# Four attentions of a transformer kernel: one counter for each cleared buffer, GpSimd's clears behind VectorE's first norms, and the centring of one weight moved to an earlier stage

## The chip, the cores and the metric

The kernel runs on 1 core of one Trainium2 chip. A core has five engines, each with an instruction stream of its own: TensorE (matmuls and transposes, results in PSUM), VectorE, ScalarE, GpSimd (which doesn't reach PSUM here) and SyncE (which issues DMAs). They are synchronised by semaphores alone: an instruction increments one when it is done, another engine waits until it has reached a number. The metric is the device time of one execution in microseconds.

## What is computed

A small vision transformer: 32 images, 25 tokens each, 192 channels, 12 heads of 16. A tokenizer makes the tokens, then four pairs of blocks follow, each with a residual and a LayerNorm. Four blocks matter here; they are cut to their core:

```python
# L1_ffn and L3_ffn: attention whose q, k, v projection has low-rank adapters, 2 of 8 chosen for each token
router_probs = softmax(x_flat @ W_gate.T + b_gate); top_k_weights, top_k_indices = top_k(router_probs, 2)
a_down = einsum('td,nrd->tnr', x_flat, A)
qkv = x @ W_qkv.T + b_qkv + sum over the chosen of weight * (a_down @ B_lora) * scaling
attn = softmax(q @ k.T * scale); return (attn @ v) @ W_proj.T + b_proj
...
# L2_attn: no bias in qkv, and q and k are normed for each head
def _norm_unbiased(t):
    mu = t.mean(-1); var = ((t - mu) ** 2).sum(-1) / (d - 1); return (t - mu) / sqrt(var)
q = _norm_unbiased(q); k = _norm_unbiased(k)
attn = softmax(q @ k.T * scale); return (attn @ v) @ proj_w.T + proj_b
...
# L3_attn: plain attention with biases
h = _layernorm(h + block(h))      # around each block
```

The subtraction of the mean in `_norm_unbiased` is done on the weights: since q and k are linear in x without a bias, centring each head's 16 columns of the weight centres every q and k.

## The kernel before

The program is nine stages, one after another. Each is a `tw.stage`, at whose end the stage's semaphores are cleared and all engines meet in a barrier (line 84). Stage 4 is L1_ffn, stage 5 L2_attn, stage 6 a mixture of experts (L2_ffn), stage 7 L3_attn, stage 8 L3_ffn. The function `attention` is called four times: as "adapted" for stages 4 and 8, as "unit" for stage 5 and as "biased" for stage 7.

The residual `tw.y` lies in SBUF as 8 tiles of 128 rows (4 images of 32 rows, 25 of them tokens). An attention handles them in four pairs, software-pipelined by one loop over i on each engine; the order on each engine is as the code is written.

- **Norm.** In a unit or biased stage VectorE norms tile t (`norm(t)`, line 759, `tensor_scalar` from `tw.y` into h): tiles 0 and 1 first, then it clears hT's rows behind the channels (line 764), sets one of them to ones (766), does the same for outT (774, 776), and then enters the loop, where the norms of later tiles are. TensorE transposes h (615), ScalarE stores the transposed tokens into hT (878; it waits for `ones_ready` 1), and TensorE projects q and k (628) and v (670). In an adapted stage a function `front` has normed and transposed all tiles before (2045, 2065, 2081), for the routing.
- **Adapters.** In an adapted stage TensorE first multiplies with the adapters' `down` weights (623, into bank_b), VectorE multiplies the result with the routing weights into mixT (785, `mix_adapters`), and the projections read mixT.
- **Clears.** Buffers whose padding must be zero are cleared by GpSimd at the start of each of these stages: qT (961), v_heads (962), probs (963), and mixT (965) in an adapted stage or top (967) in the others. All count up one semaphore, `cleared`, and whoever writes into one of these buffers first waits for `cleared` 4: VectorE in `mix_adapters`, `store_values` (818, v_heads) and `shift` (825, top and probs), ScalarE in `store_queries` (906, 907, qT) and `store_values` (916, v_heads). In a unit stage VectorE writes qT (801, 802), and GpSimd has one further job, a product into kd (974).
- **Centring.** In the unit stage VectorE centres the weights w["qk"] in place, between the memsets of hT and outT (769, 771, 773). TensorE's first projection there waits for `centred` 3.
- **Keys.** kd holds k times a mask of heads (789): from PSUM in adapted and biased stages, from SBUF in the unit stage.

`front` of stage 4 has this order on VectorE: eight norms, then a wait for TensorE's routing logits, then their copy (2048). Its SyncE queue loads expert weights of stage 6 meanwhile (fetch).

The functions that the diff touches:

Of the kernel before, what the change touches and what calls it, by code (L numbers as in the profile page):

```python
# [525 lines left out]
def attention(tw, name, kind, w, given=None):  # L526
# [12 lines left out]
    ones_ready, cleared, centred = tw.sem(name + "_ones"), tw.sem(name + "_cleared"), tw.sem(name + "_centred")  # L539
# [11 lines left out]
    with ExitStack() as ctx:  # L551
# [11 lines left out]
        if unit:  # L563
            mean = sb("w_mean", [HALF, HALVES * 2 * HEADS])
            square = sb("square", [P, 2, 3, PAIR_TOKENS])
            inv_std = sb("inv_std", [P, 2, 3, PAIR_TOKENS])
            k_unit = sb("k_unit", [P, 2, 2, PAIR_TOKENS])
# [39 lines left out]
        def _(pe):  # L607
# [25 lines left out]
            def project_queries_keys(f):  # L633
# [4 lines left out]
                if unit:  # L638
                    pe.wait_ge(centred, 3)
# [117 lines left out]
        def _(dve):  # L757
# [9 lines left out]
            if unit:  # L767
                by_head = w["qk"][0:HALF].rearrange("q k (h d) -> q (k h) d", d=HEAD_DIM)
                nc.vector.tensor_reduce(mean[:], by_head, AX_X, ALU.add).then_inc(centred, 1)
                dve.wait_ge(centred, 1)  # L770
                nc.vector.tensor_scalar(mean[:], mean[:], 1.0 / HEAD_DIM, None, ALU.mult).then_inc(centred, 1)
                dve.wait_ge(centred, 2)
                nc.vector.tensor_tensor(by_head, by_head, mean[:].unsqueeze(2).to_broadcast([HALF, HALVES * 2 * HEADS, HEAD_DIM]), ALU.subtract).then_inc(centred, 1)
# [4 lines left out]
            def mix_adapters(f):  # L778
                dve.wait_ge(down_in_psum, f + 1)
                dve.wait_ge(cleared, 4)  # L780
# [11 lines left out]
            def store_keys(f):  # L792
# [4 lines left out]
                if unit:  # L797
                    dve.wait_ge(inverse, 2 * f + 2)
                    nc.vector.tensor_tensor(k_unit[:, f % 2, 0], ps_k[0], inv_std[:, f % 2, 1], ALU.mult).then_inc(k_first, 1)
                    nc.vector.tensor_tensor(k_unit[half:P, f % 2, 1], ps_k[1], inv_std[half:P, f % 2, 2], ALU.mult).then_inc(k_scaled, 1)  # L800
                    nc.vector.tensor_tensor(qT[:, f % 2, 0, :, 0:TOKENS], by_image(ps_q[0]), by_image(inv_std[:, f % 2, 0]), ALU.mult)
# [9 lines left out]
            def store_values(t):  # L811
                dve.wait_ge(v_in_psum, t + 1)
                dve.wait_ge(cleared, 4)
# [7 lines left out]
            def shift(t):  # L821
                dve.wait_ge(scores_in_psum, t + 1)
                dve.wait_ge(cleared, 4)
# [47 lines left out]
        def _(act):  # L871
# [29 lines left out]
            def store_queries(f):  # L901
                act.wait_ge(a_in_psum, f + 1)
                act.wait_ge(cleared, 4)
# [5 lines left out]
            def store_values(t):  # L909
                act.wait_ge(v_in_psum, t + 1)  # L910
                act.wait_ge(cleared, 4)
# [48 lines left out]
        def _(pool):  # L960
            nc.gpsimd.memset(qT[:], 0.0).then_inc(cleared, 1)
            nc.gpsimd.memset(v_heads[:], 0.0).then_inc(cleared, 1)
            nc.gpsimd.memset(probs[:], 0.0).then_inc(cleared, 1)
            if adapted:
                nc.gpsimd.memset(mixT[:], 0.0).then_inc(cleared, 1)
            else:
                nc.gpsimd.memset(top[:], 0.0).then_inc(cleared, 1)
# [2229 lines left out]
```

## Time and profile before

| | us |
|---|---|
| median of 3 runs | 1129.33 |
| lowest and highest of them | 1123.27, 1134.41 |
| the profiled execution | 1121.96 |
| span of its instructions | 1120.2 |
| mean granted TensorE clock in it | 0.840 |
| busy: TensorE, VectorE, ScalarE, GpSimd | 859.2, 526.2, 333.2, 261.7 |

Times in the rows below are us from the first instruction of the profiled execution. The granted clock is a share of full speed: 1.00 is 2.4 GHz, 0.50 is 1.2 GHz. Stage 4 starts at about 599.7, stage 5 at 686.4, stage 7 at 957.8 and stage 8 at about 1025. In the profile stages 5 and 7 both name their buffers L_attn..., stages 4 and 8 L_ffn...; they are told apart by their times. PE is TensorE, PEld its loading of weights, DVE is VectorE, ACT ScalarE, POOL GpSimd and SP SyncE.

### The profile page before, as it was taken

The page shows a single profiled execution, that of the slowest core. Times are in us where ns is not written, and L with a number is a line of the kernel's source. Part 1 is how long each engine was busy: PE and PEld are TensorE (multiplying, and loading weights), DVE is VectorE, ACT ScalarE, POOL GpSimd, SP SyncE. Part 2 cuts the span into 40 slices and gives each one's busy share as a digit, 9 for nine tenths or more (in the row PEclk, how much of TensorE's full clock was granted, in tenths as well). Part 3 has the DMA queues.
Part 4 walks back from the last instruction along what each step waited for, and adds up shares of the span by engine and source line. Part 5 has one row for each costly group of instructions (what it writes and reads, how often), then busy time and mean ns, then how long its engine had stood idle before and what let it go on. Part 6 is the DMA issues. An engine that isn't in the chain of part 4 may idle for free. (4 is left out here: it accounts for less than half of the span.)

```text
span 1120.2 us, 31081 instructions
## 1 busy us (share of the span) xinstructions
PE 859.2 (77%) x13412; PEld 717.6 (64%) x13412; DVE 526.2 (47%) x1168; ACT 333.2 (30%) x677; POOL 261.7 (23%) x289
## 2 busy tenths in 40 slices
PE   8889985999629926898855795777779995587594
PEld 5578863887518925787755674565379995465472
DVE  0559973444354236655523365462731110564464
ACT  0247742122202212443442233343102221233132
POOL 1068850421133314311100101110032232100100
PEclk9989997777659966999966797796869998597698
DMA  9049967300175220000005000000428962000000
GB/s 269 10 104 178 182 120 262 142 1 1 54 231 194 89 67 1 2 3 2 1 1 190 3 4 1 2 3 9 146 62 256 296 187 28 18 4 1 2 4 24
DMA packets 56914, 88.29 MB, mean 79 GB/s; under 512 B 10756, under 2 KB 45000, under 8 KB 54756
## 3 DMA queue, kind: packets, MB, share of 16 engines
q1 hardware_dynamic: 51684, 81.85, 25.1%
q0 software_dynamic: 5120, 4.88, 2.3%
q8 instruction: 80, 1.31, 0.5%
q14 instruction: 30, 0.25, 0.1%
HBM read 78.30 MB, written 7.30 MB: 76 GB/s over the span
## 5 line engine op out<-in xcount | busy, mean ns | idle before, releaser
L2678 DVE TENSOR_TENSOR L_ffnhid<-L_ffnact_gate,L_ffnbank_u 128x300 f32<-128x300 f32 x32 | 15.0, 467 | 100.2 <-ACT L_ffnact_gate L2697 86.2
L1718 PE MATMUL ps_places<-stage_own_y,stage_spread 80*64 80x128 f32 x800 | 55.7, 288 | 2.4 <-issue 2.4
L1808 POOL TENSOR_SCALAR stage_hat_x<-stage_hat_x 128x320 f32<-128x320 f32 x40 | 51.2, 1279 | 19.9 <-ACT stage_hat_x L1784 19.9
L1868 DVE TENSOR_TENSOR stage_product<-ps_rows,stage_hat_x 128x960 f32<-128x960 f32 x40 | 46.3, 1157 | 17.9 <-PE ps_rows L1729 14.9
L1729 PE MATMUL ps_rows<-stage_strip,stage_hat_y 64*32 64x96 f32 x3200 | 49.7, 254 | 2.5 <-issue 1.7
L1718 PEld LDWEIGHTS ps_places<-stage_own_y,stage_spread 80*64 80x64 f32 x800 | 45.5, 142 | 8.6 <-issue 3.1
L1729 PEld LDWEIGHTS ps_rows<-stage_strip,stage_hat_y 64*32 64x32 f32 x3200 | 40.4, 108 | 10.1 <-issue 10.1
L2514 PE MATMUL L_ffnbank_g<-L_ffnxT,L_ffn_win 128*128 128x100 f32 (+1 forms) x184 | 46.2, 335 | 0.0
L1816 POOL TENSOR_TENSOR stage_hat_x<-stage_rel_x,stage_w_column 128x160 f32<-128x160 f32 x80 | 35.1, 460 | 45.8 <-POOLq L1523 45.8
L1873 DVE TENSOR_REDUCE stage_samples<-stage_product 128x120 f32<-128x960 f32 x40 | 45.7, 1144 | 0.0
L2515 PE MATMUL L_ffnbank_u<-L_ffnxT,L_ffn_win 128*128 128x100 f32 (+1 forms) x184 | 44.1, 324 | 0.0
L2615 POOL DMA_INDIRECT stage_y_rows<-L_ffndown,stage_choice_index x16 | 25.4, 1589 | 75.4 <-DMA stage_y_rows<-L_ffndown,stage_choice_index 46.6
L1111 PE MATMUL L_attnbank_q<-L_attnhT,L_attnwq 128*128 128x200 f32 x192 | 38.7, 343 | 5.1 <-DVE L_attnqT L1276 5.0
L1782 ACT ACTIVATE stage_hat_y<-ps_places,stage_w_minus_row 128x640 f32<-128x640 f32 x40 | 31.9, 797 | 34.8 <-PE ps_places L1718 34.8
L1111 PEld LDWEIGHTS L_attnbank_q<-L_attnhT,L_attnwq 128*128 128x128 f32 x192 | 32.3, 191 | 8.0 <-issue 7.5
L2056 POOL IOTA stage_countdown<- 128x8 f32 x3 | 0.4, 143 | 155.9 <-SPq L2036 97.4
L2522 PE MATMUL L_ffnbank_u<-L_ffnxT,L_ffn_win 64*128 64x100 f32 (+1 forms) x184 | 34.8, 333 | 1.2 <-ACT L_ffnxT L2457 0.7
L1458 POOL TENSOR_TENSOR L_attnk_norm<-L_attnk_norm,minus_half 128x12 f32<-128x12 f32 x8 | 18.2, 2270 | 72.9 <-DVE L_attnk_norm L1268 72.9
L2523 PE MATMUL L_ffnbank_g<-L_ffnxT,L_ffn_win 64*128 64x100 f32 (+1 forms) x184 | 34.9, 334 | 0.0
L2514 PEld LDWEIGHTS L_ffnbank_g<-L_ffnxT,L_ffn_win 128*128 128x128 f32 x184 | 31.7, 207 | 4.4 <-issue 3.1
L2515 PEld LDWEIGHTS L_ffnbank_u<-L_ffnxT,L_ffn_win 128*128 128x128 f32 x184 | 33.0, 208 | 1.0
L1548 PE MATMUL ps_conv<-stage_offset_w,stage_patches 128*80 128x256 f32 x120 | 29.3, 401 | 5.3 <-DMA stage_patches<-in_patchesT 5.3
(435 smaller groups left out, 2213.2 us busy)
## 6 DMA issues: line engine op xcount, KB each, us to landing
stage_strip<-in_strips SPq DMA_DIRECT2D x80, 189.0 KB
L_ffn_win<-in_L_ffn_Win SPq DMA_DIRECT2D x10, 1152.0 KB
stage_L_ffn_win<-in_L_ffn_Win SPq DMA_DIRECT2D x6, 1152.0 KB, 7.6
L_ffnranks<-stage_ranks SPq DMA_DIRECT2D x16, 400.0 KB
L_ffn_win<-in_L_ffn_Win SPq DMA_DIRECT2D x8, 768.0 KB
L_ffn_wout<-in_L_ffn_Wout SPq DMA_DIRECT2D x10, 576.0 KB
stage_L_ffn_wout<-in_L_ffn_Wout SPq DMA_DIRECT2D x6, 576.0 KB, 5.8
L_ffn_wout<-in_L_ffn_W SPq DMA_DIRECT2D x8, 384.0 KB
```

What stands on the lines that cost most here:

```text
L1111: mm = nc.tensor.matmul(bank_q[:, i * PAIR_TOKENS:(i + 1) * PAIR_TOKENS], wq[:, k, c * GROUPS + g, :], tokens, start=(k == 0), stop=(k == 1))
L1718: mm = nc.tensor.matmul(ps_places[HALF_P * h:HALF_P * (h + 1), p % 2, g * P:(g + 1) * P], k.spread[:, p * GRID + g, :], places[:, h * P:(h ...
L1729: mm = nc.tensor.matmul(ps[out, p % 2, h, g * cols:(g + 1) * cols], hat_y[rows, p, g, out], strip[rows, p, :, :, left:left + WINDOW_X].rea ...
L1782: nc.scalar.activation(y, places_in_psum(i % 2), ACT.Abs, bias=w["minus_row"][:]).then_inc(s["hat_y_abs"], 1)
L1808: nc.gpsimd.tensor_scalar(x, x, 1.0, 1.0, ALU.min, ALU.subtract).then_inc(s["hat_x"], 1)
L1816: last = nc.gpsimd.tensor_tensor(hat_x[:, p, h * GRID * IMG_PER_TILE:(h + 1) * GRID * IMG_PER_TILE, :].rearrange("q (g j) x -> q g j x", j ...
L1868: nc.vector.tensor_tensor(products(i % 2), in_psum(i % 2), weights_x(i % BUFFERS), ALU.mult).then_inc(s["multiplied"], 1)
L1873: nc.vector.tensor_reduce(into.rearrange("q h c w -> q h w c"), products(i % 2), AX_X, ALU.add, negate=True).then_inc(s["summed"], 1)
L2514: pe.matmul(gate[:, f, :], w[:, at], xT[:, 0, :], **flags)
L2515: mm = pe.matmul(up[:, f, :], w[:, self.hidden + at.start:self.hidden + at.stop], xT[:, 1, :], **flags)
L2522: pe.matmul(up[:, f, :], w[low, own], xT[low, 0, :], **flags)
L2523: mm = pe.matmul(gate[:, f, :], w[high, own], xT[high, 1, :], **flags)
```

## The change

1. The one counter `cleared` becomes four: `mix_cleared`, `q_cleared`, `v_cleared` and `probs_cleared`. Each reader waits for the buffer that it writes.
2. GpSimd clears mixT first in an adapted stage. In a unit or biased stage it waits for `ones_ready` 2, VectorE's last memset, before it clears anything.
3. In the unit stage VectorE waits for `q_cleared` before it writes qT.
4. The three centring instructions leave the unit stage. They are now on VectorE in the `front` of stage 4, behind the eight norms and ahead of the wait for the logits, and TensorE's wait for `centred` in `attention` is gone.

```diff
-    ones_ready, cleared, centred = tw.sem(name + "_ones"), tw.sem(name + "_cleared"), tw.sem(name + "_centred")
+    ones_ready = tw.sem(name + "_ones")
+    mix_cleared, q_cleared, v_cleared, probs_cleared = (tw.sem(name + x) for x in ("_mix_cleared", "_q_cleared", "_v_cleared", "_probs_cleared"))
...
         if unit:
-            mean = sb("w_mean", [HALF, HALVES * 2 * HEADS])
...
-                if unit:
-                    pe.wait_ge(centred, 3)
...
-            if unit:
-                by_head = w["qk"][0:HALF].rearrange("q k (h d) -> q (k h) d", d=HEAD_DIM)
-                nc.vector.tensor_reduce(mean[:], by_head, AX_X, ALU.add).then_inc(centred, 1)
-                dve.wait_ge(centred, 1)
-                nc.vector.tensor_scalar(mean[:], mean[:], 1.0 / HEAD_DIM, None, ALU.mult).then_inc(centred, 1)
-                dve.wait_ge(centred, 2)
-                nc.vector.tensor_tensor(by_head, by_head, mean[:].unsqueeze(2).to_broadcast([HALF, HALVES * 2 * HEADS, HEAD_DIM]), ALU.subtract).then_inc(centred, 1)
             nc.vector.memset(outT[HALF:P], 0.0).then_inc(ends_cleared, 1)
             dve.wait_ge(ends_cleared, 1 if adapted else 2)
...
             def mix_adapters(f):
                 dve.wait_ge(down_in_psum, f + 1)
-                dve.wait_ge(cleared, 4)
+                dve.wait_ge(mix_cleared, 1)
...
                     nc.vector.tensor_tensor(k_unit[half:P, f % 2, 1], ps_k[1], inv_std[half:P, f % 2, 2], ALU.mult).then_inc(k_scaled, 1)
+                    dve.wait_ge(q_cleared, 1)
                     nc.vector.tensor_tensor(qT[:, f % 2, 0, :, 0:TOKENS], by_image(ps_q[0]), by_image(inv_std[:, f % 2, 0]), ALU.mult)
...
             def store_values(t):
                 dve.wait_ge(v_in_psum, t + 1)
-                dve.wait_ge(cleared, 4)
+                dve.wait_ge(v_cleared, 1)
...
             def shift(t):
                 dve.wait_ge(scores_in_psum, t + 1)
-                dve.wait_ge(cleared, 4)
+                dve.wait_ge(probs_cleared, 1 if adapted else 2)
...
             def store_queries(f):
                 act.wait_ge(a_in_psum, f + 1)
-                act.wait_ge(cleared, 4)
+                act.wait_ge(q_cleared, 1)
...
             def store_values(t):
                 act.wait_ge(v_in_psum, t + 1)
-                act.wait_ge(cleared, 4)
+                act.wait_ge(v_cleared, 1)
...
         @block.gpsimd
         def _(pool):
-            nc.gpsimd.memset(qT[:], 0.0).then_inc(cleared, 1)
-            nc.gpsimd.memset(v_heads[:], 0.0).then_inc(cleared, 1)
-            nc.gpsimd.memset(probs[:], 0.0).then_inc(cleared, 1)
             if adapted:
-                nc.gpsimd.memset(mixT[:], 0.0).then_inc(cleared, 1)
+                nc.gpsimd.memset(mixT[:], 0.0).then_inc(mix_cleared, 1)
             else:
-                nc.gpsimd.memset(top[:], 0.0).then_inc(cleared, 1)
+                pool.wait_ge(ones_ready, 2)
+            nc.gpsimd.memset(qT[:], 0.0).then_inc(q_cleared, 1)
+            nc.gpsimd.memset(v_heads[:], 0.0).then_inc(v_cleared, 1)
+            nc.gpsimd.memset(probs[:], 0.0).then_inc(probs_cleared, 1)
+            if not adapted:
+                nc.gpsimd.memset(top[:], 0.0).then_inc(probs_cleared, 1)
 
             def store_keys(f):
...
-def front(tw, m, name, wg, experts, pair=True, fetch=None):
+def front(tw, m, name, wg, experts, pair=True, fetch=None, centre=None):
...
                                         ALU.subtract, ALU.mult).then_inc(s["normed"], 1)
+            if centre is not None:
+                mean, weights = centre
+                by_head = weights[0:HALF].rearrange("q k (h d) -> q (k h) d", d=HEAD_DIM)
+                nc.vector.tensor_reduce(mean[:], by_head, AX_X, ALU.add).then_inc(s["centred"], 1)
+                dve.wait_ge(s["centred"], 1)
+                nc.vector.tensor_scalar(mean[:], mean[:], 1.0 / HEAD_DIM, None, ALU.mult).then_inc(s["centred"], 1)
+                dve.wait_ge(s["centred"], 2)
+                nc.vector.tensor_tensor(by_head, by_head, mean[:].unsqueeze(2).to_broadcast([HALF, HALVES * 2 * HEADS, HEAD_DIM]), ALU.subtract).then_inc(s["centred"], 1)
+                dve.wait_ge(s["centred"], 3)
             dve.wait_ge(s["gated"], TILES)
             nc.vector.tensor_copy(m.logits[:, :, 0:experts], logits).then_inc(s["logits_ready"], 1)
             dve.wait_ge(s["logits_ready"], 1)
...
                 m = MoeBuffers(tw)
-                front(tw, m, l, gate[0], 8, fetch=(lambda sp: weights6.load(sp, range(3))) if l == "L1_ffn" else None)
+                first = l == "L1_ffn"
+                centre = (tw.sb("w_mean", [HALF, HALVES * 2 * HEADS]), w5["qk"]) if first else None
+                front(tw, m, l, gate[0], 8, fetch=(lambda sp: weights6.load(sp, range(3))) if first else None, centre=centre)
```

GpSimd at the start of the attention of stage 4 (L1_ffn); the names are the buffers cleared; before:

```order
L961 MEMSET L_ffnqT 128x1024
L962 MEMSET L_ffnv_heads 128x3264
L963 MEMSET L_ffnprobs 128x768
L965 MEMSET L_ffnmixT 128x512
L551 UNCONDITIONAL_BRANCH
```

GpSimd at the same place after the change, by the changed kernel's line numbers:

```order
L954 MEMSET L_ffnmixT 128x512
L957 MEMSET L_ffnqT 128x1024
L958 MEMSET L_ffnv_heads 128x3264
L959 MEMSET L_ffnprobs 128x768
L552 UNCONDITIONAL_BRANCH
```

mixT has moved from the last place to the first; stage 8 is alike.

VectorE at the start of the unit stage, stage 5, before the change (L_attnh are the normed tokens, w_mean the heads' means of the weights):

```order
L759 TENSOR_SCALAR L_attnh<-y,mean_var,rstd 128x192 x2
L764 MEMSET L_attnhT 32x1024
L766 MEMSET L_attnhT 1x2x256
L769 TENSOR_REDUCE L_attnw_mean<-w_L_attn_qk 96x48
L771 TENSOR_SCALAR L_attnw_mean<-L_attnw_mean 96x48
L773 TENSOR_TENSOR w_L_attn_qk<-w_L_attn_qk,L_attnw_mean 96x768
L774 MEMSET L_attnoutT 32x512
L776 MEMSET L_attnoutT 1x2x128
L759 TENSOR_SCALAR L_attnh<-y,mean_var,rstd 128x192
```

VectorE at the same place after the change:

```order
L757 TENSOR_SCALAR L_attnh<-y,mean_var,rstd 128x192 x2
L762 MEMSET L_attnhT 32x1024
L764 MEMSET L_attnhT 1x2x256
L765 MEMSET L_attnoutT 32x512
L767 MEMSET L_attnoutT 1x2x128
L757 TENSOR_SCALAR L_attnh<-y,mean_var,rstd 128x192
```

The three centring instructions have gone. The norm of the third tile stands directly behind the last memset, as before; that memset is now also what GpSimd's clears wait for.

VectorE in the front of stage 4 after the change:

```order
L2039 TENSOR_SCALAR stage_h_all<-y,mean_var,rstd 128x192 x8
L2044 TENSOR_REDUCE stage_w_mean<-w_L_attn_qk 96x48
L2046 TENSOR_SCALAR stage_w_mean<-stage_w_mean 96x48
L2048 TENSOR_TENSOR w_L_attn_qk<-w_L_attn_qk,stage_w_mean 96x768
L2051 COPY stage_logits<-L_ffnps_gate 128x8x8
```

Before, the copy followed the eight norms directly.

## Rows read from the trace of the kernel before

**Rows 1.** Timeline of stage 7 (biased): start, us, engine, line, what, [idle before <-releaser]

```profile
957.84 0.95 POOL L961 MEMSET L_attnqT<- 128x1024 f32 x1 [10.16 <-SPq L551]
957.84 1.28 ACT L937 ACT_TABLE_LOAD   x1 [1.35 <-PEq L84]
957.88 3.89 DVE L759 TENSOR_SCALAR L_attnh<-y,mean_var,rstd 128x192 f32<-128x192 f32 x2 [1.97 <-PEq L84]
958.73 2.93 POOL L962 MEMSET L_attnv_heads<- 128x3264 f32 x1
...
963.69 0.58 ACT L878 COPY L_attnhT<-L_attnbank_h 96x512 f32<-96x512 f32 x1 [4.57 <-DVE L_attnhT L766]
964.25 0.27 DVE L776 MEMSET L_attnoutT<- 1x256 f32 x1
...
964.32 1.70 PE L628 MATMUL L_attnbank_b<-L_attnhT,w_L_attn_qk 128*128 128x200 f32 x4 [1.42 <-ACT L_attnhT L878]
...
970.09 0.67 ACT L916 COPY L_attnv_heads<-L_attnbank_h 25x204 f32<-25x204 f32 x2 [0.81 <-PE L_attnbank_h L670]
970.34 0.38 DVE L759 TENSOR_SCALAR L_attnh<-y,mean_var,rstd 128x192 f32<-128x192 f32 x1
```

**Rows 2.** Timeline of the start of stage 5 (unit)

```profile
686.46 3.88 DVE L759 TENSOR_SCALAR L_attnh<-y,mean_var,rstd 128x192 f32<-128x192 f32 x2 [1.80 <-PEq L84]
...
692.21 0.95 DVE L769 TENSOR_REDUCE L_attnw_mean<-w_L_attn_qk 96x48 f32<-96x768 f32 x1
692.27 0.58 ACT L878 COPY L_attnhT<-L_attnbank_h 96x512 f32<-96x512 f32 x1 [4.57 <-DVE L_attnhT L766]
...
693.41 0.95 DVE L773 TENSOR_TENSOR w_L_attn_qk<-w_L_attn_qk,L_attnw_mean 96x768 f32<-96x768 f32 x1
...
694.51 1.67 PE L628 MATMUL L_attnbank_b<-L_attnhT,w_L_attn_qk 128*128 128x200 f32 x4 [3.02 <-DVE w_L_attn_qk L773]
...
695.42 0.38 DVE L759 TENSOR_SCALAR L_attnh<-y,mean_var,rstd 128x192 f32<-128x192 f32 x1
...
700.34 0.67 ACT L916 COPY L_attnv_heads<-L_attnbank_h 25x204 f32<-25x204 f32 x2 [0.89 <-PE L_attnbank_h L670]
```

**Rows 3.** The lines of the norms in attentions and in fronts, ns min/median/max

```profile
L759 DVE TENSOR_SCALAR L_attnh<-y,mean_var,rstd x16: 368/378/2945, 686.5 to 997.0; 128x192 f32<-128x192 f32 x16
...
L2045 DVE TENSOR_SCALAR stage_h_all<-y,mean_var,rstd x32: 366/374/380, 292.4 to 1027.2; 128x192 f32<-128x192 f32 x32
```

**Rows 4.** Timeline of the start of the attention in stage 4 (adapted)

```profile
622.57 0.95 POOL L961 MEMSET L_ffnqT<- 128x1024 f32 x1 [22.68 <-SPq L551]
...
622.61 1.67 PE L623 MATMUL L_ffnbank_b<-stage_hT_all,w_L_ffn_down 97*128 97x200 f32 x4 [1.93 <-PEq L2184]
...
626.90 0.52 POOL L965 MEMSET L_ffnmixT<- 128x512 f32 x1
627.53 0.37 DVE L785 TENSOR_TENSOR L_ffnmixT<-L_ffnbank_b,stage_spread 128x200 f32<-128x200 f32 x1 [3.92 <-POOL L_ffnmixT L965]
...
634.45 0.67 ACT L916 COPY L_ffnv_heads<-L_ffnbank_h 25x204 f32<-25x204 f32 x2 [0.72 <-PE L_ffnbank_h L674]
```

**Rows 5.** Waits for the clear of mixT, whole program: us in total, times, longest

```profile
DVE L_ffnmixT L785 <- POOL L_ffnmixT L965: 7.8, 2, 3.9
```

**Rows 6.** The products into kd (line 789) in stages 5 and 7, ns min/median/max

```profile
L789 DVE TENSOR_TENSOR L_attnkd<-L_attnk_unit,w_head_mask x4: 1364/1366/1376, 707.3 to 750.9; 64x800 f32<-64x800 f32 x4
...
L789 DVE TENSOR_TENSOR L_attnkd<-L_attnbank_a,w_head_mask x4: 993/993/993, 969.3 to 1004.7; 64x800 f32<-64x800 f32 x4
```

**Rows 7.** Timeline: VectorE's copy of the logits in stage 4's front

```profile
609.88 0.23 DVE L2048 COPY stage_logits<-L_ffnps_gate 128x64 f32<-128x64 f32 x1 [7.71 <-PE L_ffnps_gate L2074]
```

**Rows 8.** Windows: us, busy and count of PE, PEld, DVE, ACT, POOL, then PEclk, DMA share, GB/s

```profile
628.00:632.00 4.00, 4.00 (x13) 4.00 (x14) 0.99 (x1) 0.00 (x0) 0.00 (x0) 0.53 0.00 0
...
968.00:972.00 4.00, 2.36 (x96) 1.79 (x98) 2.49 (x5) 1.21 (x4) 0.00 (x0) 0.79 0.00 0
...
990.00:1024.00 34.00, 25.20 (x629) 18.52 (x628) 21.94 (x62) 13.91 (x35) 0.00 (x0) 1.00 0.01 3
```

More of the change, by code:

```diff
@@ L2027, in tokenizer @@
     project_and_norm(tw, k, w, load_late)
-def front(tw, m, name, wg, experts, pair=True, fetch=None):
+def front(tw, m, name, wg, experts, pair=True, fetch=None, centre=None):
     nc = tw.nc
-    s = {k: tw.sem("front_" + k) for k in "normed hT_in_psum hT_ready gated logits_ready".split()}
+    s = {k: tw.sem("front_" + k) for k in "normed centred hT_in_psum hT_ready gated logits_ready".split()}
     with nc.psum_tensor(name + "ps_hT", [HALF, 2, 512], F32) as ps_hT, \
```

## The prediction

> **What bounds the kernel now.** One core works through nine stages one after another, and each of them ends in a barrier, so a microsecond gained at the head of a stage is kept unless something inside that stage waits for a fixed point in time. Only the heads of four attention stages change, so I read the timeline of the first 10 us of each, then the waits there, then single lines for undisturbed durations, and last the granted clock.
>
> The reader is to see three delays there. First, in the two stages that norm their own tokens ("biased" from 957.8, "unit" from 686.4), VectorE's first two norms take 3.89 and 3.88 us together [rows 1, 2], while of 16 norms of that line the median takes 378 ns and the slowest 2945 ns, and the same norm in the fronts never more than 380 ns [rows 3]. The slow ones lie beside GpSimd's clears: the first norm is done when the clear of qT is (0.95 us), the second when the clear of v_heads is (957.84 + 0.95, then 2.93 us up to 961.66, against the norms' end at 961.77) [rows 1]. Second, in the unit stage TensorE's first projection also waits for the centring of w["qk"]: hT is stored at 692.27 + 0.58 = 692.85, the matmuls start at 694.51, released by L773, the last of the three centring steps [rows 2]. Third, in the two adapted stages VectorE has the adapters' product ready in PSUM at 622.61 + 1.67 = 624.28, yet multiplies only at 627.53, since it waits for all four clears and the last, mixT, ends at 627.42: 3.92 us idle [rows 4], and 7.8 us in two such waits over the program, so the second adapted stage has the same [rows 5].
>
> **Adapted stages, two of them.** mixT is cleared first: 622.57 + 0.52 = 623.09, ahead of the product at 624.28. The multiplication then starts when TensorE is done, some 0.04 later as in other waits, at 624.32 instead of 627.53: 3.21 us. The clears of qT, v_heads and probs now end 0.52 later each but still all by 627.42. The first that needs one behind the multiplication is ScalarE's copy into v_heads, at 634.45 - 3.21 = 631.24 [rows 4], so that reordering costs nothing; were v_heads behind it, the delay would be what it lacks of the 4 us of cover. Both stages: 6.42 us.
>
> **Biased stage.** GpSimd now stands behind ones_ready = 2, so nothing is beside the two norms: 2 x 0.374 = 0.75 us [rows 3], from 957.88 to 958.63 instead of 961.77, 3.14 us. What is late next? ScalarE's first copy waits for TensorE's transposes (about 1.1 us behind the norms, 959.7), its own table load (957.84 + 1.28 = 959.12) and the row of ones of hT, the last of the three: it came 1.9 us behind the norms and will again (963.69 - 3.14 = 960.55) [rows 1]. So 3.14 us arrive at TensorE's first projection.
>
> What is queued behind GpSimd's new wait are its four clears alone. VectorE's last memset ended at 964.25 + 0.27 = 964.52 [rows 1] and will at 961.38; qT is clear at 962.33, v_heads at 961.38 + 3.82 = 965.20, probs and top, smaller than qT together, within another 0.95, by 966.15: 4.8 us for the four at most. ScalarE's copy into v_heads is due at 970.09 - 3.14 = 966.95, VectorE's next norm at 970.34 - 3.14 = 967.20 [rows 1]. Cover: 1.75 us for v_heads, 1.0 us before a norm could be stopped again.
>
> New neighbours: VectorE's first multiplication into kd (one operand in PSUM) now runs beside the clear of v_heads. No row shows that pair. The nearest one is the unit stage's kd product, two operands in SBUF beside GpSimd's own product: 1366 ns, against 993 for the same size from PSUM [rows 6]. So it costs between nothing and 0.37 us. I take nothing, since in that row GpSimd reads SBUF too and a clear reads nothing, and keep 0.4 for the range. (The Trainium skill, "SBUF — State Buffer", section "Who interferes with whom", says that a VectorE instruction with at most one SBUF input, outside the two-port modes, does not contend with GpSimd, and one with two SBUF inputs only with a GpSimd instruction that reads. By it the term is 0, by the nearest row 0.4.)
>
> **Unit stage.** The norms again: 686.46 + 0.75 = 687.21 instead of 690.34, 3.13 us. The centring leaves as well: TensorE then starts behind hT, at 692.90 instead of 694.51 on the old scale, another 1.61 us. Together 4.74: the first projection at 689.77.
>
> Here the third norm (0.38 us at 695.42 [rows 2]) stands right behind the memsets, so it now meets GpSimd's first clear. At worst it waits for the clear of qT and that of v_heads, 3.9 us, until about 693.9, and it is not needed before VectorE's copy at 700.34 - 4.74 = 695.60 [rows 2]; TensorE turns those tokens later still. If the norm goes first, the clears start 0.38 late: v_heads is clear at 690.0 + 3.82 + 0.38 = 694.2, 1.4 us ahead of the copies at 695.60. Either way 0. (This is where a rule speaks against the change: the same page and section says that whichever starts first keeps the shared ports for its whole instruction and the other fully blocks, so a norm can again lose 2.9 us here, as the 2945 ns of [rows 3] agree. By that rule the norm's delay is 3.9 us at most; on the chain it is hidden either way.)
>
> **The centring in the front** of the first adapted stage: 692.21 to 693.41 + 0.95 = 694.36, 2.15 us with the waits between the steps [rows 2], in VectorE's idle 7.71 us before it copies the logits [rows 7]. 5.5 us of cover are left, TensorE and ScalarE do not wait for VectorE there after the norms. Cost 0. Without the cover it would be 2.15 us.
>
> **Clock.** In the first adapted stage the granted clock goes from 1.2 to 2.4 GHz at about 631.8 (mean 0.53 in 628 to 632), 3.8 us after the projections start at 627.95; in the biased one at 969.7 (0.79 in 968 to 972), 5.4 us after its start at 964.32 [rows 8, 1]. If the rise only moves with the work, nothing is added. If the adapters' product, now 0.46 us instead of 3.67 ahead of the projections, counts towards it, up to 2.1 us of work goes from one level to the other; at half the time for it that is 1.05 per adapted stage. I take 1.0 for both together; ends 0 and 2.1. Where in the work the rise falls also scatters by 1.6 us between these stages, worth 0.8 us per stage, 3.2 over four, either sign, and it does so from run to run.
>
> **Sum.** 6.42 + 3.14 + 4.74 + 1.0 = 15.3 us. More semaphores are cleared at the stages' ends, but the instruction rows there are unchanged; 0. Against the profiled execution (1121.96) it gives 1106.7. That execution is 0.65% below the median of the runs, 1129.33, by which a change is judged; the stages that the sum takes from do not depend on the difference, so I forecast 1129.33 - 15.3 = **1114.0 us**.
>
> **Rivals.**
> (a) *The norms are slow for another reason*, such as being the first instructions behind a barrier. Against: in the fronts they are that too, at 374 ns. Then 6.4 + 1.6 + 1.0 = 9.0 us are left: 1120.3. Chance 0.05.
> (b) *The late clears become the wait*: clears and VectorE's work stretch each other, and the copies into v_heads wait for v_cleared in the unit and biased stages. It decides from 1.75 us late (1.4 in the unit stage). If the 4.8 us of clears doubled, the copies would be about 3 us late twice: 15.3 - 6 = 9.3 us, 1120.0. For it speaks that clears and norms did hold each other up; against it, that only one norm meets them now. Chance 0.09.
> (c) *The clock turns against it, slower than before*: the shorter pauses and shifted work cost the biased stage its long high stretch, 34 us from 990 to 1024 at 1.00 with 25.2 us of TensorE busy [rows 8]. At 1.2 GHz that work takes up to twice as long, 50.4 us, 16.4 more than the stretch has even if its idle 8.8 us are filled, and more than the 15.3 gained: 1114.0 + 16.4 = 1130.4. It decides from the point where 93% of that stretch is low. In the unit stage the level does go up and down in every pair, which speaks for it; that the change puts more work into the same time speaks against. Chance 0.03.
> (d) My forecast, all four heads short: 0.83.
>
> **Numbers.** The forecast's own spread is the clock's 3.2, the bounds 0.4 and 1.1 (and 1.0 if nothing is gained by the clock), and the median of three runs that lie 1123.27 to 1134.41, some 4 us; with (a) and (b), which lie inside, 1106 to 1122 should hold 8 in 10. A measurement of this kernel can tell about 1% from no change, 11.3 us: 1118.0. The forecast clears it by 4 us, some 86% of its cases: 0.71; the rest of it, (a), (b) and most of the mild form of (c) are within 1%: 0.27; slower by over 1% only a stronger (c): 0.02.
>
> **What would show it.** Right: in the profile after, the first two norms of the unit and biased stages take under 0.8 us; the multiplication into mixT waits for TensorE and not for GpSimd; TensorE's first projection lies 3.1 to 3.2 us closer to the start of the stage (4.7 in the unit stage) and waits for hT; the front's logits copy starts as long after the norms as before. Wrong: a wait of ScalarE or VectorE for v_heads or qT, a third norm of the unit stage that holds up the copies, or pairs at 1.2 GHz that were at 2.4.

## The result, and the profile after

The changed kernel takes 1108.89 us (median of 4 executions, 1106.48 to 1114.48) against 1130.01 before (4 executions on the same chip, 1123.27 to 1134.41): ratio 0.985, 95% interval 0.9802 to 0.9898. A second measurement of the same two kernels, e8 below, gives 0.9841 (0.9785 to 0.9897). These ratios are estimated over the fast executions and are not the quotient of the two medians, which is 0.981 here. The forecast was 1114.0 us, a ratio of 0.986, in a range of 1106 to 1122. The profiled execution took 1110.26 us.

Line numbers of the changed kernel differ from those before by a few: its norms are L757, the copy of hT L870, the product into mixT L776, the products into kd L780.

Timeline of the start of the unit stage in the changed kernel, against [rows 2]:

```profile
692.44 0.67 DVE L757 TENSOR_SCALAR L_attnh<-y,mean_var,rstd 128x192 f32<-128x192 f32 x2 [1.81 <-PEq L84]
...
695.03 0.58 ACT L870 COPY L_attnhT<-L_attnbank_h 96x512 f32<-96x512 f32 x1 [1.35 <-DVE L_attnhT L764]
...
695.67 1.70 PE L628 MATMUL L_attnbank_b<-L_attnhT,w_L_attn_qk 128*128 128x200 f32 x4 [1.41 <-ACT L_attnhT L870]
695.90 1.09 DVE L757 TENSOR_SCALAR L_attnh<-y,mean_var,rstd 128x192 f32<-128x192 f32 x1
695.92 0.95 POOL L957 MEMSET L_attnqT<- 128x1024 f32 x1 [60.37 <-DVE L_attnoutT L767]
696.82 2.92 POOL L958 MEMSET L_attnv_heads<- 128x3264 f32 x1
...
700.61 0.66 ACT L908 COPY L_attnv_heads<-L_attnbank_h 25x204 f32<-25x204 f32 x2 [0.32 <-PE L_attnbank_h L668]
```

The first two norms take 0.67 us together instead of 3.88, and TensorE's projection now waits for ScalarE's copy of hT, no longer for the centring. From the first norm to the first projection it is 695.67 - 692.44 = 3.23 us, where it was 694.51 - 686.46 = 8.05: 4.82 less, against 4.74 forecast. The third norm is the one that now meets a clear: 1.09 us instead of 0.38, hidden as it stood in the prediction. GpSimd's v_heads is clear at 699.74, 0.87 us before ScalarE's copy at 700.61, which still waits for TensorE.

The biased stage, against [rows 1]:

```profile
952.90 0.67 DVE L757 TENSOR_SCALAR L_attnh<-y,mean_var,rstd 128x192 f32<-128x192 f32 x2 [1.97 <-PEq L84]
...
956.12 1.70 PE L628 MATMUL L_attnbank_b<-L_attnhT,w_L_attn_qk 128*128 128x200 f32 x4 [1.41 <-ACT L_attnhT L870]
956.38 0.95 POOL L957 MEMSET L_attnqT<- 128x1024 f32 x1 [13.60 <-DVE L_attnoutT L767]
957.27 2.82 POOL L958 MEMSET L_attnv_heads<- 128x3264 f32 x1
...
957.86 0.99 DVE L780 TENSOR_TENSOR L_attnkd<-L_attnbank_b,w_head_mask 128x800 f32<-128x800 f32 x1 [1.54 <-PE L_attnbank_b L628]
...
962.07 0.66 ACT L908 COPY L_attnv_heads<-L_attnbank_h 25x204 f32<-25x204 f32 x2 [1.00 <-PE L_attnbank_h L668]
```

3.22 us from norm to projection where it was 6.44, so 3.22 less (forecast 3.14). The product into kd lies wholly beside the clear of v_heads and takes 0.99 us, as it does without a neighbour: of the bounds 0 and 0.37 for it, 0 holds. That clear is done at 960.09, 2.0 us ahead of its first reader.

The adapted attention of stage 4, against [rows 4]:

```profile
630.70 0.52 POOL L954 MEMSET L_ffnmixT<- 128x512 f32 x1 [23.01 <-POOLq L2187]
...
630.74 1.67 PE L623 MATMUL L_ffnbank_b<-stage_hT_all,w_L_ffn_down 97*128 97x200 f32 x4 [1.93 <-PEq L2187]
...
632.45 0.37 DVE L776 TENSOR_TENSOR L_ffnmixT<-L_ffnbank_b,stage_spread 128x200 f32<-128x200 f32 x1 [0.71 <-PE L_ffnbank_b L623]
...
632.87 1.37 PE L628 MATMUL L_ffnbank_b<-stage_hT_all,w_L_ffn_qk 97*128 97x200 f32 x3 [0.46 <-DVE L_ffnmixT L776]
```

VectorE's idle time before the multiplication fell from 3.92 to 0.71 us and is ended by TensorE. Adapters to projection: 2.13 us instead of 5.34, 3.21 less to the hundredth, and the same 2.13 in stage 8. The centring in the front, against [rows 7]:

```profile
609.90 0.94 DVE L2044 TENSOR_REDUCE stage_w_mean<-w_L_attn_qk 96x48 f32<-96x768 f32 x1
...
611.09 0.96 DVE L2048 TENSOR_TENSOR w_L_attn_qk<-w_L_attn_qk,stage_w_mean 96x768 f32<-96x768 f32 x1
...
617.99 0.22 DVE L2051 COPY stage_logits<-L_ffnps_gate 128x64 f32<-128x64 f32 x1 [5.95 <-PE L_ffnps_gate L2077]
```

5.95 us of idle time are left where 7.71 were. From the front's first norm to this copy it is 10.42 us, against 10.11 before; that 0.3 is mostly TensorE's clock, see "Hidden costs" below.

The line of all norms and two windows of granted clock in the changed kernel, against [rows 3] and [rows 8]:

```profile
L757 DVE TENSOR_SCALAR L_attnh<-y,mean_var,rstd x16: 369/376/1087, 692.4 to 987.3; 128x192 f32<-128x192 f32 x16
...
636.00:640.00 4.00, 3.82 (x106) 3.44 (x105) 1.08 (x2) 0.66 (x3) 0.00 (x0) 0.78 0.00 0
...
980.00:1016.00 36.00, 25.59 (x633) 18.92 (x632) 22.45 (x64) 13.86 (x35) 0.14 (x1) 1.00 0.01 3
```

The slowest of the 16 norms is 1087 ns, no longer 2945. The long stretch at 2.4 GHz of the biased stage is still there.

By the heads alone the change is worth 3.21 + 3.21 + 3.22 + 4.82 = **14.46 us**. The medians differ by 21.1, and the profiled executions by 11.7. What stands between is the subject of a table behind the experiments.

### The profile page after: what moved, and what is told of

It reads as the page before. It is cut to its first block and busy times, and to the rows that moved or that the text cites. A ratio compares the mean times of both kernels' runs of the same rounds, so it can differ in the third digit from the quotient of the medians.

```text
span 1108.5 us, 31081 instructions
## 1 busy us (share of the span) xinstructions
PE 860.5 (78%) x13412; PEld 720.2 (65%) x13412; DVE 522.3 (47%) x1168; ACT 332.2 (30%) x677; POOL 261.2 (24%) x289
## 5 line engine op out<-in xcount | busy, mean ns | idle before, releaser
L1862 DVE TENSOR_TENSOR stage_product<-ps_rows,stage_hat_x 128x960 f32<-128x960 f32 x40 | 46.3, 1158 | 13.9 <-PE ps_rows L1723 11.9
L1105 PE MATMUL L_attnbank_q<-L_attnhT,L_attnwq 128*128 128x200 f32 x192 | 42.7, 369 | 6.9 <-DVE L_attnqT L1270 6.7
L1105 PEld LDWEIGHTS L_attnbank_q<-L_attnhT,L_attnwq 128*128 128x128 f32 x192 | 36.3, 210 | 9.5 <-issue 8.7
L1144 PE MATMUL L_attnbank_o<-L_attnv_heads,L_attnwork 128*100 128x68 f32 x192 | 26.3, 315 | 16.2 <-ACT L_attnwork L1396 15.0
L1144 PEld LDWEIGHTS L_attnbank_o<-L_attnv_heads,L_attnwork 128*100 128x100 f32 x192 | 25.1, 226 | 18.2 <-ACT L_attnwork L1396 16.2
```

Source lines behind the costliest of these rows:

```text
L1105: mm = nc.tensor.matmul(bank_q[:, i * PAIR_TOKENS:(i + 1) * PAIR_TOKENS], wq[:, k, c * GROUPS + g, :], tokens, start=(k == 0), stop=(k == 1))
L1144: mm = nc.tensor.matmul(bank_o[0:QUERIES, j // 2, at:at + OUT_COLS], work[:, t % 2, j * GROUPS + g, :], v_heads[:, t % 4, j, g, :, :], sta ...
L1862: nc.vector.tensor_tensor(products(i % 2), in_psum(i % 2), weights_x(i % BUFFERS), ALU.mult).then_inc(s["multiplied"], 1)
```

## The experiments

"Head" is the time from the first norm of a unit or biased stage to TensorE's first projection there, or from the adapters' first matmul to the first projection in an adapted stage. It is read from the trace to a hundredth, where the total can't tell changes of a few us: the kernel before alone ranges from 1116.36 to 1136.02 over its executions here.

**e1: counters alone.** The kernel before with four counters and mixT first; GpSimd doesn't wait, the centring stays.

```diff
             if adapted:
                 nc.gpsimd.memset(mixT[:], 0.0).then_inc(mix_cleared, 1)
-            else:
-                pool.wait_ge(ones_ready, 2)
             nc.gpsimd.memset(qT[:], 0.0).then_inc(q_cleared, 1)
```

(The diff is against the changed kernel; the centring is put back as before.)

> The kernel before with one part alone: four counters, mixT cleared first. GpSimd clears at once as before and the centring stays in the unit stage. My theory: the adapted stages' multiplication into mixT waits for TensorE instead of GpSimd, 5.34 us from TensorE's first adapter matmul to its first projection become 2.13 in each of the two; the heads of the unit and biased stages stay as before (8.05 and 6.44 us from the first norm to the first projection). Time 6.4 us below before, about 1123.5. Rival: the second adapted stage's start is bound otherwise and only one of them gains, 3.2 us.

Median 1118.49 against 1126.03, ratio 0.9894 (0.9834 to 0.9953). Timeline of stage 4:

```profile
629.94 0.52 POOL L964 MEMSET L_ffnmixT<- 128x512 f32 x1 [22.90 <-POOLq L2186]
...
631.69 0.37 DVE L786 TENSOR_TENSOR L_ffnmixT<-L_ffnbank_b,stage_spread 128x200 f32<-128x200 f32 x1 [0.71 <-PE L_ffnbank_b L624]
...
632.11 1.70 PE L629 MATMUL L_ffnbank_b<-stage_hT_all,w_L_ffn_qk 97*128 97x200 f32 x4 [0.46 <-DVE L_ffnmixT L786]
```

Both adapted heads fall to 2.13 and 2.14, those of the unit and biased stages stay at 8.05 and 6.45. The ratio says 11.9 us with an interval of 5.3 to 18.7, which holds 6.4. The rival, one stage alone, falls. The run changes both the counters and the order of the clears. Neither was run by itself; by [rows 4] neither would gain alone, since with one counter the last clear, and with the old order mixT's own, ends at 627.42 all the same.

**e2: late clears alone.**

```diff
         def _(pool):
+            if not adapted:
+                pool.wait_ge(ones_ready, 2)
             nc.gpsimd.memset(qT[:], 0.0).then_inc(cleared, 1)
```

> The kernel before with one part alone: GpSimd waits for ones_ready 2 in the unit and biased stages. Theory of the ports: the two first norms take 0.7 us instead of 3.9, the biased head 6.44 becomes 3.22; in the unit stage the centring still stands between, and GpSimd's clears begin only behind it, head 8.05 becomes 4.85. One counter for all clears: v_heads' copies now wait for the last clear, 4.6 us behind GpSimd's start; with 1.7 us of cover in the biased stage it is reached within 0.2 us, in the unit stage it has to hold up the copies by 0 to 1 us. Time 6.3 us below before. Rival (slow first instructions): nothing changes at the norms, time as before or slower.

Median 1121.56 against 1126.03, ratio 0.9973 (0.993 to 1.0015): 3.0 us, interval -1.7 to 7.9; 6.3 lies in it, no gain as well. The trace is clearer: heads 4.84 and 3.23, so 3.21 us gained at each. What the single counter costs shows in the biased stage:

```profile
975.70 0.13 POOL L969 MEMSET L_attntop<- 128x24 f32 x1
975.91 0.33 ACT L906 COPY L_attnqT<-L_attnbank_a 64x200 f32<-64x200 f32 x1 [4.86 <-POOL L_attntop L969]
```

ScalarE's first copy into qT waits for the clear of top, a buffer that it has nothing to do with, and starts 975.91 - 971.11 = 4.80 us after the first projection instead of 4.40 in the changed kernel. It was this copy, not the one into v_heads that I had expected, and in the unit stage nothing waited. So with one counter the late clears made this copy 0.4 us later, and with four no copy is late. The stage's length doesn't show the 0.4: it is 62.65 us here and 62.59 and 62.71 in the changed kernel (table below).

**e3: centring alone.**

```diff
-            if unit:
-                by_head = w["qk"][0:HALF].rearrange("q k (h d) -> q (k h) d", d=HEAD_DIM)
...
+                centre = (tw.sb("w_mean", [HALF, HALVES * 2 * HEADS]), w5["qk"]) if first else None
```

> The kernel before with one part alone: the centring in the front of stage 4. Theory: the unit stage's head goes from 8.05 to 6.44 us, the biased stage's value, since the two then have the same work in it; the front's logits copy comes 10.1 us behind the first norm as before, with 5.6 to 6.0 us of VectorE's idle time left before it. Rival: the front gets longer by up to 2.2 us, because VectorE is later for its copy, and the gain is given back.

One execution, 1120.46. In the unit stage:

```profile
696.12 3.89 DVE L756 TENSOR_SCALAR L_attnh<-y,mean_var,rstd 128x192 f32<-128x192 f32 x2 [1.78 <-PEq L84]
...
702.57 1.70 PE L627 MATMUL L_attnbank_b<-L_attnhT,w_L_attn_qk 128*128 128x200 f32 x4 [1.42 <-ACT L_attnhT L868]
```

Head 6.45, 1.60 less. The logits copy comes 10.42 us behind the front's first norm, with 5.95 us of idle time ahead of it. The rival, up to 2.2 us given back in the front, falls.

**e4: the first two clears swapped,** in the kernel before.

```diff
-            nc.gpsimd.memset(qT[:], 0.0).then_inc(cleared, 1)
             nc.gpsimd.memset(v_heads[:], 0.0).then_inc(cleared, 1)
+            nc.gpsimd.memset(qT[:], 0.0).then_inc(cleared, 1)
```

> The kernel before with GpSimd's first two clears swapped: v_heads (2.9 us) first, then qT (0.95 us). If each norm waits for the clear that runs and is let in between two clears, the first norm now takes 2.9 to 3.0 us and the second 1.0, both together 3.9 as before. If the norms are slow for a reason of their own, the first stays at 1.0 and the second at 2.9. If a norm is stopped for as long as GpSimd works at all, both end only behind all clears.

One execution, 1125.75. A window that holds only the first norm, and GpSimd's clears:

```profile
694.74 2.88 DVE L759 TENSOR_SCALAR L_attnh<-y,mean_var,rstd 128x192 f32<-128x192 f32 x1 [1.79 <-PEq L84]
...
694.70 2.82 POOL L961 MEMSET L_attnv_heads<- 128x3264 f32 x1 [60.46 <-POOLq L84]
694.74 3.88 DVE L759 TENSOR_SCALAR L_attnh<-y,mean_var,rstd 128x192 f32<-128x192 f32 x2 [1.79 <-PEq L84]
697.46 1.06 POOL L962 MEMSET L_attnqT<- 128x1024 f32 x1
```

The first norm now takes 2.88 us, so the second has 1.0 of the 3.88 that both take. The durations have changed places with the clears. That settles it: each norm waits for the clear that is running, and is let in before the next; rival (a) of the prediction, slow first instructions, would have left the first at 1.0. The clear behind a norm pays a little too: v_heads takes 2.82 us here as first and 2.93 in [rows 1] as second, qT 1.06 as second and 0.95 there as first.

**e5: another form of the norm,** in the kernel before, early clears. Only the first two norms of each stage are changed; they compute the same values.

```diff
-                norm(0)
-                norm(1)
+                norm_by_row(0)      # scalar_tensor_tensor(h, y, mean, rstd broadcast, subtract, mult)
+                norm_by_row(1)
```

> The kernel before with the first two norms of the unit and biased stages written as scalar_tensor_tensor (the same values; rstd as a broadcast tensor), GpSimd's clears at once as before. If the norms wait because tensor_scalar takes a port that GpSimd uses, this form (two operands in SBUF beside a clear that reads nothing) isn't stopped: both norms 0.7 to 0.9 us together beside the clears, heads 3.2 us shorter. If every VectorE instruction that reads SBUF is stopped by a clear, or the first instructions behind a barrier are slow, the two still take 3.9.

One execution, 1124.35. In the unit stage:

```profile
700.22 0.95 POOL L964 MEMSET L_attnqT<- 128x1024 f32 x1 [60.16 <-POOLq L84]
...
700.28 0.74 DVE L762 SCALAR_TENSOR_TENSOR L_attnh<-y,mean_var,rstd 128x192 f32<-128x192 f32 x2 [1.80 <-PEq L84]
...
701.11 2.82 POOL L965 MEMSET L_attnv_heads<- 128x3264 f32 x1
...
703.87 0.78 DVE L774 TENSOR_SCALAR L_attnw_mean<-L_attnw_mean 96x48 f32<-96x48 f32 x1
703.87 0.74 POOL L966 MEMSET L_attnprobs<- 128x768 f32 x1
```

Both norms are done in 0.74 us while GpSimd clears qT. It is the form `tensor_scalar` that is stopped, not VectorE at large, and not the place behind the barrier. A second case, not planned, is in the last two rows: the centring's tiny `tensor_scalar` over 48 columns, 0.18 us elsewhere, takes 0.78 here. It begins together with the clear of probs and ends at 704.65, just behind that clear's end at 704.61. (The Trainium skill, "SBUF — State Buffer", section "Who interferes with whom", has this as a rule: `tensor_scalar` can enter a two-port mode and then contends with any GpSimd instruction, while an instruction with two SBUF inputs contends only with one that reads. e4 and e5 agree with both halves.) The biased head is 3.30 us, so a changed form is worth nearly what the late clears are, 3.14 against 3.21. The unit head is 5.51 us, 2.54 less and not the 3.2 expected; the missing 0.60 us are what that tiny `tensor_scalar` now loses.

**e6: how much cover the late clears have.** The changed kernel, with v_heads cleared twice.

```diff
+            if not adapted:
+                nc.gpsimd.memset(v_heads[:], 0.0).then_inc(v_once, 1)
+                pool.wait_ge(v_once, 1)
             nc.gpsimd.memset(v_heads[:], 0.0).then_inc(v_cleared, 1)
```

> The changed kernel, with v_heads cleared twice in the unit and biased stages, so that its counter comes 2.8 us later. By the changed kernel's trace v_heads is clear 2.0 us before ScalarE's first copy in the biased stage and 0.9 to 1.0 before it in the unit stage (there with TensorE at the higher clock for a part of it). Theory: the copies now wait for GpSimd, 0.8 us in the biased stage and 1 to 1.9 us in the unit stage, and the work behind them comes later by as much; heads up to the first projection stay at 3.23. Rival: more cover than that, since the copies are not on the chain; no wait, nothing later.

One execution, 1113.4. In the unit stage:

```profile
698.86 1.70 PE L628 MATMUL L_attnbank_b<-L_attnhT,w_L_attn_qk 128*128 128x200 f32 x4 [1.42 <-ACT L_attnhT L870]
...
702.99 2.82 POOL L961 MEMSET L_attnv_heads<- 128x3264 f32 x1
...
705.90 0.66 ACT L908 COPY L_attnv_heads<-L_attnbank_h 25x204 f32<-25x204 f32 x2 [2.28 <-POOL L_attnv_heads L961]
...
706.82 1.67 PE L652 MATMUL L_attnbank_h<-L_attnsquare,w_same_head 128*128 128x200 f32 x4 [2.95 <-DVE L_attnv_heads L810]
```

The copy comes 7.04 us behind the first projection instead of 4.94: 2.10 late, where the clear ended 2.88 us later, so some 0.8 of cover. In the biased stage ScalarE's copy starts at 967.28, released by the second clear, where the values had been in PSUM from 965.95: 1.2 us late. This is the wait of rival (b) made to happen, and the changed kernel doesn't reach it.

What the lateness costs differs. In the unit stage it costs more than itself: TensorE stands idle for 2.95 us instead of 0.97, the granted clock is 1.00 up to about 706 and 0.50 behind that, the matmuls L652 take 1.67 us instead of the 0.92 of the changed kernel, and the second pair's projection comes 17.40 us behind the first instead of 13.55. The stage takes 84.28 us against 80.36 and 80.77. In the biased stage nothing of the 1.2 us is seen in the stage's 62.84. Both are of one execution.

**e7: a shorter clear ahead of the first copy.** The changed kernel, with hT's rows cleared one buffer after the other, and GpSimd behind the norms.

```diff
-                nc.vector.memset(hT[HALF:P], 0.0).then_inc(ends_cleared, 1)
-                dve.wait_ge(ends_cleared, 1)
-                nc.vector.memset(hT[HALF:HALF + 1, :, 0], 1.0).then_inc(ones_ready, 1)
+                for x in range(2):
+                    nc.vector.memset(hT[HALF:P, x], 0.0).then_inc(ends_cleared, 1)
+                    dve.wait_ge(ends_cleared, x + 1)
+                    nc.vector.memset(hT[HALF:HALF + 1, x, 0], 1.0).then_inc(ones_ready, 1)
...
-                pool.wait_ge(ones_ready, 2)
+                pool.wait_ge(normed, 2)
```

> The changed kernel with hT's clearing split, the first pair's half first (0.48 and 0.27 us in place of 0.91 and 0.48), so that ScalarE's first copy waits for half as much, and with GpSimd's clears behind the two norms instead of behind the last memset. Theory: heads of the unit and biased stages 3.23 to about 2.6 us, 1.3 us in all, which the total can't show against its scatter; the third norm of the unit stage meets the clear of v_heads and takes 2 to 3 us, hidden. Rival: the clears that run beside VectorE's memsets stretch them or the copy, and nothing is gained.

Median 1108.91 against 1124.98, ratio 0.9834 (0.9786 to 0.9882). In the biased stage:

```profile
939.52 0.67 DVE L757 TENSOR_SCALAR L_attnh<-y,mean_var,rstd 128x192 f32<-128x192 f32 x2 [1.97 <-PEq L84]
...
941.37 0.58 ACT L871 COPY L_attnhT<-L_attnbank_h 96x512 f32<-96x512 f32 x1 [0.61 <-PE L_attnbank_h L615]
...
942.00 1.70 PE L628 MATMUL L_attnbank_b<-L_attnhT,w_L_attn_qk 128*128 128x200 f32 x4 [0.67 <-ACT L_attnhT L871]
```

Heads 2.43 and 2.48 us: 0.80 and 0.74 less. In the biased stage the copy now waits for TensorE's transposes, so the memsets are off the path; in the unit stage, where the transposes took 0.64 us at 2.4 GHz instead of 1.09, it still waits for the memset (L765). The memsets keep their 0.48 and 0.27 us beside the clears, so the rival falls. The third norm of the unit stage took 0.97, not the 2 to 3 that I expected, since the clear was almost over by then. In the total the 1.5 us don't show: against e8 on the same chip it is the same.

**e8: the changed kernel again.**

> The changed kernel once more, unchanged, against the kernel before on the same chip. Theory: the four heads gain 14.5 us by the two traces, with the clock in between some 15 to 16, ratio 0.986; the median moves by less than 0.3% from its first measurement. If the first measurement's 21 us were right as they stand, the ratio comes out at 0.981.

Median 1107.84 against 1124.98 (6 and 10 executions), ratio 0.9841 (0.9785 to 0.9897). The heads are 2.13, 3.22, 3.23 and 2.13 again. The ratio lies between the two values named, and the interval holds both.

**Where the rest of the difference is.** The stage times in all ten traces, from the first norm of a stage to that of the next (stage 8 to the end of the span), and the start of stage 4, up to which all kernels are the same:

| us | start of 4 | stage 4 | stage 5 | stage 6 | stage 7 | stage 8 |
|---|---|---|---|---|---|---|
| before | 599.77 | 86.69 | 84.95 | 186.47 | 67.30 | 95.02 |
| after | 607.57 | 84.87 | 80.36 | 180.10 | 62.59 | 93.01 |
| e8, after | 606.83 | 84.36 | 80.77 | 179.97 | 62.71 | 92.16 |
| e1, counters | 606.92 | 84.82 | 86.94 | 179.57 | 66.61 | 92.14 |
| e2, late clears | 611.40 | 87.59 | 84.45 | 184.44 | 62.65 | 95.47 |
| e3, centring | 608.14 | 87.98 | 83.97 | 179.01 | 65.25 | 94.35 |
| e4, swapped | 606.36 | 88.38 | 86.87 | 180.49 | 65.85 | 96.05 |
| e5, norm form | 612.18 | 88.10 | 84.11 | 178.85 | 63.43 | 95.93 |
| e6, cover | 611.05 | 84.58 | 84.28 | 177.22 | 62.84 | 91.63 |
| e7, split | 600.08 | 82.43 | 79.00 | 178.01 | 63.33 | 90.75 |

Stage 4 takes 84.66 on average in the four traces with mixT first (e7, with a clock of its own, left out) and 87.75 in the five without: 3.1 us. Stage 8, by the same traces: 92.2 and 95.4, 3.1 us. Stage 7: 62.65 with late clears (after, e8, e2) and 66.25 untouched (before, e1, e3, e4): 3.6. Stage 5: 80.6 in the changed kernel and 86.25 untouched (before, e1, e4): 5.7. Together **15.5 us**. The parts that no edit touches scatter by more than any of these: 12.4 us up to the start of stage 4, 9.3 us in stage 6. In the heads alone the three parts add up without a rest: 3.21 + 3.20 (e1), 3.21 + 3.21 (e2) and 1.60 (e3) are 14.43 of the 14.46.

## Why the prediction was right

**Sizes.** All four heads came out within 0.08 us of the forecast: 3.21 for 3.21 twice, 3.22 for 3.14, 4.82 for 4.74. The two 0.08 are the norms, which I had taken as 2 x 0.374 while two in a row overlap and take 0.67.

**The clock term** of 1.0 us, for an earlier rise in the adapted stages, isn't borne out. In the profile after, the clock rises at about 637.8 (0.78 in 636 to 640), 4.9 us behind the projection's start at 632.87, not 3.8 or less. The 3.8 was peculiar to one trace: with mixT last it is 5.1 to 5.2 us in e2 to e5, with mixT first 4.9 to 5.0 in e1, e6 and e8 (6.5 in e7, where the level fell from 2.4 to 1.2 GHz just ahead of the projection). So the rise moves with the work, all but some 0.2 us. Stages 4 and 8 fell by 3.1 us, the head's gain and no more. Its place in the sum is taken by 0.9 us beyond the head in stage 5 and 0.4 in stage 7. For stage 7 nothing shows that this is an effect.

In the unit stage, for whose clock the prediction took no gain, the traces do show one. The values' matmuls of its second tile and the second pair's projection, before and after:

```profile
703.41 1.59 PE L670 MATMUL L_attnbank_h<-w_L_attn_v,L_attnhT 128*32 128x51 f32 x64 [0.92 <-ACT L_attninv_std L896]
...
709.60 1.70 PE L628 MATMUL L_attnbank_b<-L_attnhT,w_L_attn_qk 128*128 128x200 f32 x4
```

```profile
703.68 0.93 PE L668 MATMUL L_attnbank_h<-w_L_attn_v,L_attnhT 128*32 128x51 f32 x64 [0.91 <-ACT L_attninv_std L888]
...
709.22 1.70 PE L628 MATMUL L_attnbank_b<-L_attnhT,w_L_attn_qk 128*128 128x200 f32 x4
```

From the first pair's projection to the second's it is 15.09, 15.11 and 15.07 us in the untouched unit stages (before, e1, e4) and 13.55, 13.80 and 13.80 with the centring gone (after, e8, e3), 1.3 to 1.6 us less. The granted clock rises 5.5 to 5.6 us behind the first projection in the former and 3.5 to 4.0 in the latter, and the second tile's value matmuls take 0.93 us, at 2.4 GHz, instead of 1.59. TensorE had stood idle for 3.02 us ahead of the first projection in the former, 1.42 in the latter. That the shorter pause is the cause isn't shown: in e2 and e5, with pauses of 3.02 and 3.62, the distance is 14.54 and 14.12 us.

**The total** was forecast 5 us above the first measurement. The trace-by-trace sum of 15.5 us against the forecast's 15.3, and ratios of 0.985 and 0.984 against 0.986, say that the sum was right in size and that the 21 us between 1130.01 and 1108.89 are partly scatter: the medians of the kernel before in the two later comparisons were 1126.03 and 1124.98. By the ratios the change is worth 17 to 18 us with an interval of some 6 to each side. That sum and stage times agree to 0.2 us is luck as well: the forecast's 1.0 for the adapted stages stands where the runs have a gain in the unit stage.

**Hidden costs.** Each cover that the prediction named was there. mixT first: nobody waited for a later clear (e1). Late clears: none waited in the changed kernel, and e6 shows the point at which one would. The cover was 2.0 us in the biased stage, against 1.75 forecast, but in the unit stage only 0.9 against 1.4, since with the earlier rise of the clock the values are ready 4.94 us behind the projection and not 5.83 as before. The third norm of the unit stage took 1.09 us: it waited for the one clear of 0.95 us and lost 0.7, not the 3.9 named as the worst. Centring in the front: 5.95 us of idle time left. A small part of it is not fully hidden: in fronts that start at 1.2 GHz the logits copy comes 10.34 or 10.35 us behind the first norm without the centring (e1, e2, e4, e5) and 10.42 with it (after, e3, e6, e8). TensorE's last matmul for it ends 10.31 us behind the first norm in e1 and 10.32 in e3, so the 0.07 us lie between that and VectorE's start; their cause is open. (The 10.11 of the kernel before had the first 1.3 us of its front at 2.4 GHz.)

**Rivals.** (a) falls by e4 and e5. (b)'s wait is real, but needs another 0.9 us of clears in the unit stage and 1.6 to 2.0 in the biased one (after, e6). (c) didn't happen: 36 us of the biased stage, 980 to 1016, ran at a granted clock of 1.00, as 34 did before. Its mechanism wasn't forced in this stage, so it stays unlikely rather than refuted; that a longer pause of TensorE goes with a lower level is seen in e6's unit stage, in one execution.

## What to carry to other kernels

A short instruction that is slow only at one place is best explained by its neighbour's duration: 1.02 and 2.95 us for norms of 0.37 were the lengths of GpSimd's two clears, 0.95 and 2.93, to 0.07 us. Work of GpSimd at the head of a stage can be moved behind VectorE's first `tensor_scalar`, or the instruction written in a form that isn't stopped, as long as its first reader is later than its end; count that cover in us before. A reader that comes late can cost more than its wait, when TensorE's clock falls in the pause, as it did in e6's one execution. And one counter for several producers makes each reader wait for the last of them: a counter each, with the first-needed buffer cleared first, gave 3.2 us twice, and no wait behind it showed a cost.

## What the runs showed of the hardware

- GpSimd's clears and VectorE's `tensor_scalar` norms take turns instruction by instruction: the waiting norm is let in after one clear, not after all (2.88 and 1.0 us in e4), and the clear behind it is 0.11 us longer (2.82 to 2.93, 0.95 to 1.06).
- A `tensor_scalar` over 48 columns waits for a whole clear too: 0.78 us instead of 0.18, beside the clear of probs of 0.74 (e5). The same norms as `scalar_tensor_tensor` don't wait: two in 0.74 us.
- VectorE's memsets (0.48 and 0.27 us beside GpSimd's clears in e7 as elsewhere) and its product with one operand in PSUM (0.99 in the changed kernel) are not stopped or stretched.
- With the same code TensorE's mean granted clock differs from execution to execution, 0.825 to 0.848 over 22 of the kernel before. The parts that nobody touched vary by 9 to 12 us in 1120, so that a single pair of executions can't tell the 15 us of this change, while heads read from one trace each repeat to 0.01 us.
